# First attention layer: where GpSimd's low parts, the value load and the early expert parts stand

## The chip, the cores and the metric

The kernel runs on one core of a Trainium2 chip. The metric is the device time of one execution in microseconds (us). Five engines work side by side and wait for each other by semaphores: TensorE (PE), VectorE (DVE), ScalarE (ACT), GpSimd (POOL) and SyncE (SP, which here issues the DMA transfers).

## The reference

Two transformer layers over 2 sequences of 512 tokens, width 256. Each is attention, then a mixture of 16 experts. Only the first attention layer (16 heads of size 128) is touched by the change:

```python
x = x + _L0_attn_ref(_layernorm(x), ...)
# per head: q, k, v = x @ W + b; q, k = rotary(q), rotary(k)
scores = where(causal, q @ k.T / sqrt(128), 0)
max_v  = max(abs(scores), axis=-1)
attn_w = sign(scores) * exp(sign(scores) * scores - max_v)
attn   = attn_w / (sum(abs(attn_w)) + 1e-6)
out    = (attn @ v) @ W_O + b_O
x = x + _L0_ffn_ref(_layernorm(x), ...)      # experts, top 4 of 16, and a shared one
x = x + _L1_attn_ref(_layernorm(x), ...)
x = x + _L1_ffn_ref(_layernorm(x), ...)
```

## The kernel before

Matrix products are done in three passes over a high and a low part of each factor (`PARTS`): ScalarE rounds a float32 tile to its high part by a copy (`wqk_hi`, `wv_hi`, `wo_hi`, `ew_hi`), and GpSimd subtracts it from the raw tile to get the low part (`wqk_lo`, `wv_lo`, `wo_lo`, `ew_lo`).

The first layer is 32 heads (16 for each sequence), software-pipelined in steps i = -4 to 32. In step i TensorE projects q and k of head i+2 (L319), multiplies q by k for head i+1 (L330), applies the output weights for head i-1 (L343), transposes the weights `w` of head i (L357), projects v for two heads in halves (L370), and multiplies `w` by v for head i (L382). Steps 3 to 10 and 19 to 26 are run by a hardware loop with four steps in its body (`known(i)` is false there, since the step is a register); the others are written out one by one. After a written-out step, `a0_at_pe`, `a0_at_pool` and the like add work that belongs to that step alone.

Each engine runs its instructions strictly in program order; that order is written out by hand in `a0_pe`, `a0_act`, `a0_dve`, `a0_pool` and `a0_sp`. Around the change:

- GpSimd, `a0_pool`: L511 makes `wqk_lo` of head i+3, L518 the two products `q_sin` of the rotary step for head i+2 (from `q_sw`, q with neighbouring rows swapped by DMA), L525 masks `sabs` and `sgn` (absolute value and sign of the scores) for head i+1, L530 makes `wo_lo` of head i, L534 `wv_lo` of head i+4. In steps 28 to 30 `a0_at_pool` adds the low part `ew_lo` of an expert's weights, behind a wait for `rden`, and in step -3 the normalization's `rstd` of the second sequence (`ln_pool`, L265).
- VectorE, `a0_dve`: L468 and L474 finish the rotary step (`q_rot`), L479 takes the row maxima `nmax`, L486 multiplies `ex` by a mask and sums it into `den`, L458 adds the bias of v, L493 and L495 make `rden`, L499 the low part `z_lo`, L505 `w = ex * rden * sgn` in four pieces of 512, 384, 128 and 256 columns.
- SyncE, `a0_sp`: four swaps `q_sw`, then the loads of `wo_raw`, `wqk_raw` and `wv_raw`, each behind a wait for the low part that frees its one buffer.
- Before the steps, TensorE is kept warm with products of ones (L644), transposes `xn` (L277), the normalized input that VectorE writes at L242, and goes on to head 0.

## Time and profile before

| | us |
|---|---|
| median of 3 runs | 871.27 |
| lowest and highest | 868.90, 878.65 |
| the profiled execution, its own time | 869.21 |
| its span in the trace | 867.5 |

In the profiled execution TensorE is busy 95% of the span, VectorE 77%, ScalarE 60% and GpSimd 54%. A row of the time line is: start, length, engine, line, operation, output<-inputs, shapes, number of instructions merged, and in brackets how long the engine had been idle and what ended that. The granted clock is that of TensorE, where 1.00 is 2.4 GHz and 0.50 is 1.2 GHz.

### The profile page before, as it was taken

What the parts mean: (1) busy time and instruction counts of PE and PEld (TensorE: products, weight loads), DVE (VectorE), ACT (ScalarE), POOL (GpSimd) and SP (SyncE); (2) the same over time, 40 slices, a digit from 0 to 9 for tenths busy, and PEclk for the clock granted to TensorE, in tenths of its full rate; (3) what the DMA queues carried; (4) which work ended last, traced back from release to release, by engine and by line L of the source; (5) the groups of instructions that cost most, each with busy time, mean ns of one, the idle gap of its engine ahead of it and who ended that gap; (6) DMA issues with size and microseconds to landing.
All of it is one profiled execution on the core that took longest, in us unless ns stands there. A gap on an engine that the chain in (4) does not pass through costs nothing.

```text
span 867.5 us, 14790 instructions
## 1 busy us (share of the span) xinstructions
PE 826.4 (95%) x4549; PEld 626.9 (72%) x4549; DVE 670.3 (77%) x1350; ACT 522.9 (60%) x1106; POOL 469.1 (54%) x399
## 2 busy tenths in 40 slices
PE   8899999999989999889998999999999989999997
PEld 6678888777878888667787888664444447888886
DVE  5799999999999999998477865868788644675554
ACT  3778888786878888763644533336566665454442
POOL 3565555665666666532575766614210526656774
PEclk9999999999999999999999999999999999999999
DMA  4323332222432223211665457412441133334451
GB/s 148 101 97 99 98 97 97 96 83 73 148 97 99 97 97 98 68 48 49 201 226 166 140 164 271 155 57 63 142 136 53 56 99 92 122 122 141 152 161 65
DMA packets 57426, 99.20 MB, mean 114 GB/s; under 512 B 8272, under 2 KB 19024, under 8 KB 57360
## 3 DMA queue, kind: packets, MB, share of 16 engines
q1 hardware_dynamic: 57360, 98.39, 35.6%
q8 instruction: 33, 0.54, 0.3%
q14 instruction: 33, 0.27, 0.1%
HBM read 71.88 MB, written 9.57 MB: 94 GB/s over the span
## 4 chain that ended last, share of the span: by engine, by line
PE 63%; DVE 11%; issue 10%; POOL 9%; ACT 4%; DMA 2%; DVEq 0%; SPq 0%; ACTq 0%; POOLq 0%
PE ps L956 10%; PE ps L942 9%; PE ps L933 9%; PE ps L319 6%; PE ps L382 5%; PE ps L330 4%; POOL q_sin L518 3%; PE ps L343 3%; PE ps L370 3%; PE ps L1505 3%; PE ps L1624 3%; PE ps L357 2%; DVE w L505 2%; PE ps L1594 2%; DVE nm L1816 2%
## 5 line engine op out<-in xcount | busy, mean ns | idle before, releaser
L1080 POOL TENSOR_TENSOR ew_lo<-ew_raw,ew_hi 128x768 fp32r<-128x768 f32 x68 | 128.1, 1884 | 64.5 <-ACT ew_hi L1046 46.0
L1032 ACT ACTIVATE hid_hi<-guw 128x512 fp32r<-128x512 f32 x68 | 43.0, 632 | 156.6 <-POOL guw L1096 106.5
L1135 DVE TENSOR_TENSOR hid_lo<-guw,hid_hi 128x512 fp32r<-128x512 f32 x68 | 80.6, 1185 | 72.4 <-ACT hid_hi L1032 72.3
L1096 POOL TENSOR_TENSOR guw<-gu,cwb 128x512 f32<-128x512 f32 x61 | 80.4, 1319 | 91.5 <-issue 74.0
L505 DVE SCALAR_TENSOR_TENSOR w<-ex,rden,sgn 128x512 f32<-128x512 f32 (+3 forms) x128 | 103.2, 866 | 0.0
L1816 DVE TENSOR_REDUCE nm<-ps 128x1 f32<-128x512 f32 x128 | 81.3, 682 | 19.9 <-PE ps L1528 18.7
L1711 ACT ACTIVATE e<-ps 128x512 f32<-128x512 f32 x128 | 68.7, 602 | 36.8 <-PE ps L1624 36.6
L518 POOL TENSOR_TENSOR q_sin<-q_sw,sin 128x512 f32<-128x512 f32 x64 | 85.6, 1354 | 3.0 <-DMA q_sw<-q_in 2.7
L433 ACT ACTIVATE ex<-sabs,nmax 128x512 f32<-128x512 f32 (+3 forms) x128 | 61.5, 552 | 36.3 <-DVE nmax L479 36.3
L956 PE MATMUL ps<-ew_hi,hid_hi 128*128 128x256 f32 x272 | 78.4, 288 | 2.4 <-DVE hid_lo L1135 1.8
L956 PE MATMUL ps<-ew_hi,hid_lo 128*128 128x256 f32 x272 | 76.9, 283 | 0.0
L956 PE MATMUL ps<-ew_lo,hid_hi 128*128 128x256 f32 x272 | 76.9, 283 | 0.0
L382 PE MATMUL ps<-wT,v 128*128 128x512 f32 (+3 forms) x256 | 74.3, 433 | 1.0 <-ACT wT L418 1.0
L330 PE MATMUL ps<-q_rot 128*128 128x512 f32 (+3 forms) x256 | 74.2, 433 | 0.0
L511 POOL TENSOR_TENSOR wqk_lo<-wqk_raw,wqk_hi 128x512 fp32r<-128x512 f32 x32 | 43.9, 1371 | 55.8 <-ACT wqk_hi L398 55.8
L382 PEld LDWEIGHTS ps<-wT,v 128*128 128x128 f32 x256 | 46.3, 190 | 26.8 <-issue 16.6
L534 POOL TENSOR_TENSOR wv_lo<-wv_raw,wv_hi 128x256 fp32r<-128x256 f32 x32 | 23.8, 744 | 74.4 <-ACT wv_hi L448 74.4
L330 PEld LDWEIGHTS ps<-q_rot 128*128 128x128 f32 x256 | 43.3, 190 | 26.4 <-issue 15.4
L392 ACT ACTIVATE q_in<-ps,bqkv 128x512 f32<-128x512 f32 x64 | 43.7, 686 | 27.9 <-PE ps L319 27.4
L474 DVE TENSOR_TENSOR q_rot<-ps,q_sin 128x512 f32<-128x512 f32 x64 | 43.5, 686 | 22.1 <-POOL q_sin L518 19.9
L410 ACT ACTIVATE sgn<-ps 128x512 bf16<-128x512 f32 (+3 forms) x128 | 60.0, 469 | 0.0
L933 PE MATMUL ps<-xT_hi,ew_hi 128*128 128x512 f32 x136 | 55.8, 410 | 3.6 <-issue 3.6
(189 smaller groups left out, 2443.4 us busy)
## 6 DMA issues: line engine op xcount, KB each, us to landing
ew_raw<-in_ew SPq DMA_DIRECT2D x68, 384.0 KB, 3.4
q_sw<-q_in SPq DMA_DIRECT2D x128, 128.0 KB, 2.0
cwb<-cw_dram SPq DMA_DIRECT2D x61, 256.0 KB, 3.6
wqk_raw<-in_wqk SPq DMA_DIRECT2D x32, 256.0 KB, 2.9
wv_raw<-in_wv SPq DMA_DIRECT2D x32, 128.0 KB, 2.7
wo_raw<-in_wo SPq DMA_DIRECT2D x32, 128.0 KB, 2.2
qs<-stk_q SPq DMA_DIRECT2D x16, 256.0 KB, 3.7
ks<-stk_k SPq DMA_DIRECT2D x16, 256.0 KB, 4.3
```

What stands on the lines that cost most here:

```text
L330: pe.matmul(ps[:, bank, col:col + P * (qi + 1)], q_rot[:, par(1), 0, qi * P:(qi + 1) * P], q_rot[:, par(1), 1, 0:P * (qi + 1)], start=True ...
L382: last = pe.matmul(ps[:, 7, j * P:S], v0[:, slot_of(0), j, odd() * DH0:(odd() + 1) * DH0], wT[:, j, j * P:S], start=j == 0, stop=j == QT - ...
L505: dve.scalar_tensor_tensor(out=w[:, qi, ROW[qi]], in0=ex[:, qi, ROW[qi]], scalar=rden[:, qi:qi + 1], in1=sgn[:, par(1), qi, ROW[qi]], op0= ...
L518: pool.tensor_tensor(q_sin[:, t, :], q_sw[:, t, :], sin0[:, :], ALU.mult).then_inc(sem("q_sin"), 1)
L933: last = pe.matmul(ps[:, gu_pair(f, i)[0], :], ff[f].ew[pw][:, i % EW_SLOTS, c * P:(c + 1) * P], half_of((xT_hi, xT_lo)[px][:, c, :], h), ...
L942: last = pe.matmul(ps[:, gu_pair(f, i)[1], :], ff[f].ew[pw][:, i % EW_SLOTS, (DC + c) * P:(DC + c + 1) * P], half_of((xT_hi, xT_lo)[px][:, ...
L956: last = pe.matmul(ps[:, Y_BANK[f, h][t // 2], t % 2 * D:(t % 2 + 1) * D], ff[f].hid[px][:, i % 2, t * P:(t + 1) * P], ff[f].ew[pw][:, i % ...
L1080: pool.tensor_tensor(ff[f].ew[1][:, i % EW_SLOTS, :], ew_raw[:, i % RAW_SLOTS, :], fp(ff[f].ew[0][:, i % EW_SLOTS, :]), ALU.subtract).then ...
L1096: pool.tensor_tensor(ff[f].guw[:, i % 2, :], ff[f].gu[:, i % 2, :], ff[f].cwb[:, r % CWB_SLOTS, :], ALU.mult).then_inc(sem("guw"), 1)
L1135: dve.tensor_tensor(ff[f].hid[1][:, i % 2, :], ff[f].guw[:, i % 2, :], fp(ff[f].hid[0][:, i % 2, :]), ALU.subtract).then_inc(sem("hid_lo"), 1)
L1711: act.activation(e1[:, s % 2 * HEADS + j, :], ps[:, S_BANK[n % S_BANKS], :], ACT.Exp, scale=SCALE1).then_inc(sem("e1"), 1)
L1816: dve.tensor_reduce(nm1[:, quad % 2, col:col + 1], ps[:, BANK_OF["max", n], :], AX.X, ALU.max, negate=True).then_inc(sem("max"), 1)
```

## The change

Five moves, no arithmetic is added or removed. (1) In the two hardware loops `wqk_lo` goes from first place in GpSimd's step to behind the two masks. (2) There, `wo_lo` gets a further wait, for the four sums `den` of head i+1. (3) In the loops, SyncE issues the load of `wv_raw` before those of `wo_raw` and `wqk_raw`. (4) At the start, `wv_lo` and `wqk_lo` of head 0 wait until the four `xn` tiles of the first sequence are written, and `rstd` of the second sequence goes ahead of `wv_lo` of head 1. (5) In steps 28 to 30 an expert's `ew_lo` goes from the end of the step, behind a wait for `rden`, to right behind the masks, without that wait, and ahead of `wo_lo` (in step 28 also ahead of `rstd`, `gw_lo` and a memset).

```diff
--- before.py
+++ after.py
@@ -504,12 +504,20 @@
                 for qi in QORDER:
                     dve.scalar_tensor_tensor(out=w[:, qi, ROW[qi]], in0=ex[:, qi, ROW[qi]], scalar=rden[:, qi:qi + 1],
                                              in1=sgn[:, par(1), qi, ROW[qi]], op0=ALU.mult, op1=ALU.mult).then_inc(sem("w"), 1)
-        def a0_pool(pool, i):
+        def wqk_low(pool, i):
             if valid(i + 3, N0):
                 n = i + 3
+                if known(i) and i == -3:
+                    pool.wait_ge(sem("xn"), QT)
                 wait(pool, "wqk_hi", n + 1)
                 pool.tensor_tensor(wqk[1][:, :, :, :], wqk_raw[:, :, :, :], fp(wqk[0][:, :, :, :]),
                                    ALU.subtract).then_inc(sem("wqk_lo"), 1)
+
+        def a0_pool(pool, i):
+            if known(i):
+                wqk_low(pool, i)
+            if known(i) and i == -3:
+                ln_pool(pool, 0, (1,))
             if valid(i + 2, N0):
                 n = i + 2
                 for t in range(2):
@@ -524,19 +532,32 @@
                     diag = t[:, :, S - P:S]
                     pool.affine_select(out=diag, in_=diag, compare_op=ALU.is_ge, fill=0.0, base=0,
                                        pattern=[[0, QT], [-1, P]], channel_multiplier=1).then_inc(sem("causal"), 1)
+            if not known(i):
+                wqk_low(pool, i)
+            if known(i) and N0 - 4 <= i <= N0 - 2:
+                ew_low(pool, 0, i - (N0 - 4))
             if valid(i, N0):
                 n = i
                 wait(pool, "wo_hi", n + 1)
+                if not known(i):
+                    wait(pool, "den", QT * (n + 2))
                 pool.tensor_tensor(wo[1][:, :], wo_raw[:, :], fp(wo[0][:, :]), ALU.subtract).then_inc(sem("wo_lo"), 1)
             if valid(i + 4, N0):
                 n = i + 4
                 wait(pool, "wv_hi", n + 1)
+                if known(i) and i == -4:
+                    pool.wait_ge(sem("xn"), QT)
                 pool.tensor_tensor(wv[1][:, slot_of(4), :, odd(), :], wv_raw[:, :, :], fp(wv[0][:, slot_of(4), :, odd(), :]),
                                    ALU.subtract).then_inc(sem("wv_lo"), 1)
 
         def a0_sp(sp, i):
             def head(n):
                 return n % H0 if known(n) else n - batch[0] * H0
+
+            def load_wv(sp, n):
+                src = a["wv0"][head(n)]
+                wait(sp, "wv_lo", n)
+                sp.dma_start(wv_raw[:, :, :], src).then_inc(sem("wv_ld"), 16)
 
             if valid(i + 2, N0):
                 n = i + 2
@@ -544,6 +565,8 @@
                     wait(sp, "q_ev", of_pair(n + 1, t))
                     for o in range(2):
                         sp.dma_start(q_sw[o:P:2, t, :], q_in[1 - o:P:2, t, :]).then_inc(sem(f"swap{t}"), 16)
+            if not known(i):
+                load_wv(sp, i + 4)
             if valid(i, N0):
                 n = i
                 src = a["wo0"][head(n)]
@@ -554,9 +577,8 @@
                 src = a["wqk0"][head(n)]
                 wait(sp, "wqk_lo", n)
                 sp.dma_start(wqk_raw[:, :, :, :], src).then_inc(sem("wqk_ld"), 16)
-                src = a["wv0"][head(n)]
-                wait(sp, "wv_lo", n)
-                sp.dma_start(wv_raw[:, :, :], src).then_inc(sem("wv_ld"), 16)
+                if known(i):
+                    load_wv(sp, n)
 
         batch = [0]
         quarter = [0]
@@ -610,7 +632,6 @@
 
         def a0_at_pool(pool, i):
             if i == -3:
-                ln_pool(pool, 0, (1,))
                 pool.wait_ge(sem("tab0"), 80)
             if H0 - 5 <= i < H0 - 1:
                 t = 2 * (i - (H0 - 5))
@@ -627,9 +648,6 @@
             if i == N0 - 4:
                 ln_pool(pool, 1, (0,))
                 gw_low(pool, 0)
-            if N0 - 4 <= i <= N0 - 2:
-                pool.wait_ge(sem("rden"), i + 2)
-                ew_low(pool, 0, i - (N0 - 4))
             if i == N0 - 2:
                 ew_low(pool, 0, 3)
             if i == N0:
```

GpSimd in the hardware loop, first of its four steps, before (L511 is `wqk_lo` of head i+3; rows of L217 set registers for the waits):

```order
L511 TENSOR_TENSOR wqk_lo<-wqk_raw,wqk_hi 128x512 [waits wqk_hi]
L217 ISA
L217 ISA [waits swap0]
L518 TENSOR_TENSOR q_sin<-q_sw,sin_66 128x512 [waits q_rot]
L217 REGISTER_ALU [waits swap1]
L518 TENSOR_TENSOR q_sin<-q_sw,sin_66 128x512 [waits q_rot]
L217 ISA
L525 AFFINE_SELECT sabs<-sabs 128x4x128 [waits sgn]
L525 AFFINE_SELECT sgn<-sgn 128x4x128
L530 TENSOR_TENSOR wo_lo<-wo_raw,wo_hi 128x256 [waits wo_hi]
L217 REGISTER_ALU
L534 TENSOR_TENSOR wv_lo<-wv_raw,wv_hi 128x2x128 [waits wv_hi]
```

and now:

```order
L526 TENSOR_TENSOR q_sin<-q_sw,sin_66 128x512 [waits q_rot]
L217 REGISTER_ALU [waits swap1]
L526 TENSOR_TENSOR q_sin<-q_sw,sin_66 128x512 [waits q_rot]
L217 ISA
L533 AFFINE_SELECT sabs<-sabs 128x4x128 [waits sgn]
L533 AFFINE_SELECT sgn<-sgn 128x4x128
L217 REGISTER_ALU
L513 TENSOR_TENSOR wqk_lo<-wqk_raw,wqk_hi 128x512 [waits wqk_hi]
L217 ISA [waits wo_hi]
L544 TENSOR_TENSOR wo_lo<-wo_raw,wo_hi 128x256 [waits den]
L217 REGISTER_ALU
L550 TENSOR_TENSOR wv_lo<-wv_raw,wv_hi 128x2x128 [waits wv_hi]
```

`wqk_lo` moved from ahead of the swaps' products to behind the masks, and `wo_lo` waits for `den` too. SyncE in the same step, before:

```order
L546 DMA q_sw<-q_in 64x512 [waits q_ev]
L546 DMA q_sw<-q_in 64x512
L217 REGISTER_ALU
L551 ISA [waits wo_lo]
L551 DMA wo_raw<-in_wo 128x256
L217 REGISTER_ALU
L556 ISA [waits wqk_lo]
L556 DMA wqk_raw<-in_wqk 128x512
L559 ISA [waits wv_lo]
L559 DMA wv_raw<-in_wv 128x256
```

and now:

```order
L567 DMA q_sw<-q_in 64x512 [waits q_ev]
L567 DMA q_sw<-q_in 64x512
L217 REGISTER_ALU
L560 ISA [waits wv_lo]
L560 DMA wv_raw<-in_wv 128x256
L217 REGISTER_ALU
L574 ISA [waits wo_lo]
L574 DMA wo_raw<-in_wo 128x256
L579 ISA [waits wqk_lo]
L579 DMA wqk_raw<-in_wqk 128x512
```

The value load moved ahead of the two others; the load of `wqk_raw` is last and waits for the `wqk_lo` that now comes later. GpSimd in steps 28 and 29, written out, before (L1080 is `ew_lo` of experts 0 and 1):

```order
L525 AFFINE_SELECT sgn<-sgn 128x4x128
L530 TENSOR_TENSOR wo_lo<-wo_raw,wo_hi 128x256 [waits wo_hi]
L265 TENSOR_TENSOR rstd<-vareps,minus_half 128x4 [waits ln_var]
L1085 TENSOR_TENSOR gw_lo<-gw_raw,gw_hi 128x32 [waits gw_hi]
L1087 MEMSET runs 128x640
L1080 TENSOR_TENSOR ew_lo<-ew_raw,ew_hi 128x768 [waits ew_hi_act,rden]
L518 TENSOR_TENSOR q_sin<-q_sw,sin_66 128x512 [waits q_rot,swap0]
L518 TENSOR_TENSOR q_sin<-q_sw,sin_66 128x512 [waits q_rot,swap1]
L525 AFFINE_SELECT sabs<-sabs 128x4x128 [waits sgn]
L525 AFFINE_SELECT sgn<-sgn 128x4x128
L530 TENSOR_TENSOR wo_lo<-wo_raw,wo_hi 128x256 [waits wo_hi]
L1080 TENSOR_TENSOR ew_lo<-ew_raw,ew_hi 128x768 [waits ew_hi_act,rden]
```

and now:

```order
L533 AFFINE_SELECT sgn<-sgn 128x4x128
L1098 TENSOR_TENSOR ew_lo<-ew_raw,ew_hi 128x768 [waits ew_hi_act]
L544 TENSOR_TENSOR wo_lo<-wo_raw,wo_hi 128x256 [waits wo_hi]
L265 TENSOR_TENSOR rstd<-vareps,minus_half 128x4 [waits ln_var]
L1103 TENSOR_TENSOR gw_lo<-gw_raw,gw_hi 128x32 [waits gw_hi]
L1105 MEMSET runs 128x640
L526 TENSOR_TENSOR q_sin<-q_sw,sin_66 128x512 [waits q_rot,swap0]
L526 TENSOR_TENSOR q_sin<-q_sw,sin_66 128x512 [waits q_rot,swap1]
L533 AFFINE_SELECT sabs<-sabs 128x4x128 [waits sgn]
L533 AFFINE_SELECT sgn<-sgn 128x4x128
L1098 TENSOR_TENSOR ew_lo<-ew_raw,ew_hi 128x768 [waits ew_hi_act]
L544 TENSOR_TENSOR wo_lo<-wo_raw,wo_hi 128x256 [waits wo_hi]
```

In each step `ew_lo` moved up to the masks and lost its wait for `rden`; in step 28 it is also ahead of L265, L1103 and L1105 (`rstd`, `gw_lo`, memset).

## Rows read from the trace of the kernel before

**Rows 1.** Windows: length, busy us of PE, PEld, DVE, ACT, POOL; clock, DMA, GB/s.

```profile
260.00:310.00 50.00, 50.00 (x279) 40.27 (x278) 47.65 (x111) 40.82 (x101) 29.48 (x31) 1.00 0.29 95
369.30:372.80 3.50, 3.50 (x18) 3.50 (x19) 3.50 (x7) 1.83 (x5) 1.40 (x3) 0.52 0.02 9
```

**Rows 2.** TensorE's waits, 40 to 400 us: total, how many, longest.

```profile
PE ps L357 <- DVE w L505: 11.0, 6, 3.5
```

**Rows 3.** Time line of TensorE, steps 5 and 6.

```profile
96.65 0.59 PE L382 MATMUL ps<-wT,v 128*128 128x512 f32 x1
98.73 0.49 PE L319 MATMUL ps<-xT_hi,wqk_hi 128*128 128x512 f32 x1
107.70 0.59 PE L382 MATMUL ps<-wT,v 128*128 128x512 f32 x1
```

**Rows 4.** Time line of VectorE, the same step.

```profile
96.27 0.69 DVE L474 TENSOR_TENSOR q_rot<-ps,q_sin 128x512 f32<-128x512 f32 x1 [0.56 <-POOL q_sin L518]
96.88 1.65 DVE L479 TENSOR_REDUCE nmax<-sabs 128x1 f32<-128x512 f32 x4
101.85 2.96 DVE L505 SCALAR_TENSOR_TENSOR w<-ex,rden,sgn 128x512 f32<-128x512 f32 x4
```

**Rows 5.** Time line of GpSimd, the same step.

```profile
93.46 2.72 POOL L518 TENSOR_TENSOR q_sin<-q_sw,sin 128x512 f32<-128x512 f32 x2
96.13 0.64 POOL L525 TENSOR_SCALAR_AFFINE_SELECT sabs<-sabs 128x512 f32<-128x512 f32 x1
97.32 0.73 POOL L530 TENSOR_TENSOR wo_lo<-wo_raw,wo_hi 128x256 fp32r<-128x256 f32 x1
...
103.18 1.34 POOL L511 TENSOR_TENSOR wqk_lo<-wqk_raw,wqk_hi 128x512 fp32r<-128x512 f32 x1 [2.07 <-ACT wqk_hi L398]
```

**Rows 6.** One line: ns min/median/max, starts; the last piece of w at two places.

```profile
L505 DVE SCALAR_TENSOR_TENSOR w<-ex,rden,sgn x1: 1506/1506/1506, 103.3 to 103.3; 128x256 f32<-128x256 f32 x1
...
L505 DVE SCALAR_TENSOR_TENSOR w<-ex,rden,sgn x1: 471/471/471, 380.9 to 380.9; 128x256 f32<-128x256 f32 x1
```

**Rows 7.** One line or tile: a step's second swap, and GpSimd's lengths, 40 to 352.

```profile
L546 SPq DMA_DIRECT2D q_sw<-q_in x2: 465/530/596, 102.6 to 103.1; - x2
DMA to landing us min/median/max: 1.9/2.0/2.1
...
L511 POOL TENSOR_TENSOR wqk_lo<-wqk_raw,wqk_hi x27: 1281/1357/1652, 46.8 to 341.1; 128x512 fp32r<-128x512 f32 x27
```

**Rows 8.** Time line of the start, TensorE and VectorE.

```profile
9.86 0.61 PE L644 MATMUL ps<-ones_r 128*128 128x512 f32 x2
10.79 1.07 PE L277 MATMUL ps<-ident,xn 128*128 128x128 f32 x8 [0.32 <-DVE xn L242]
...
7.88 2.76 DVE L242 TENSOR_SCALAR xn<-x,meanvar,rstd 128x256 f32<-128x256 f32 x4 [1.20 <-POOL rstd L265]
16.30 1.38 DVE L242 TENSOR_SCALAR xn<-x,meanvar,rstd 128x256 f32<-128x256 f32 x4 [1.13 <-POOL rstd L265]
```

**Rows 9.** Time line of steps 28 to 30: VectorE, GpSimd, TensorE.

```profile
363.93 5.23 DVE L505 SCALAR_TENSOR_TENSOR w<-ex,rden,sgn 128x512 f32<-128x512 f32 x4
369.09 2.00 DVE L242 TENSOR_SCALAR xn<-x,meanvar,rstd 128x256 f32<-128x256 f32 x4
378.20 3.16 DVE L505 SCALAR_TENSOR_TENSOR w<-ex,rden,sgn 128x512 f32<-128x512 f32 x4
...
363.52 1.83 POOL L1080 TENSOR_TENSOR ew_lo<-ew_raw,ew_hi 128x768 fp32r<-128x768 f32 x1 [3.66 <-DVE rden L495]
366.35 2.53 POOL L518 TENSOR_TENSOR q_sin<-q_sw,sin 128x512 f32<-128x512 f32 x2 [1.00 <-DMA q_sw<-q_in]
...
377.79 1.84 POOL L1080 TENSOR_TENSOR ew_lo<-ew_raw,ew_hi 128x768 fp32r<-128x768 f32 x1 [4.65 <-DVE rden L495]
...
369.22 1.19 PE L357 MATMUL ps<-ident,w 128*128 128x128 f32 x5 [3.46 <-DVE w L505]
...
381.42 1.31 PE L357 MATMUL ps<-ident,w 128*128 128x128 f32 x10 [1.25 <-DVE w L505]
```

## The prediction

> **What bounds the kernel now.** The whole change lies in the first layer, so I read that stage. The busy windows come first: over 50 us inside the second hardware loop TensorE is busy for all 50 us at clock 1.00, while VectorE has 47.65 and GpSimd 29.48 [rows 1]. The time line of TensorE gives the step: from the product with v of one head to that of the next it is 107.70 - 96.65 = 11.05 us [rows 3]. So in the loops (16 of 32 heads) TensorE has no hole that a faster partner could close. Its waits from 40 to 400 us come next: 11.0 us in six waits for `w`, the longest 3.5 us [rows 2]. Since the loops have no idle time, these lie in the steps that are written out. The reader is to see that VectorE is nearly full too, and that it is slowed by GpSimd at two kinds of place. In the loop the last piece of `w` takes 1506 ns, against 471 ns for the same piece in step 30 [rows 6]; it starts at 103.3, just behind the start of `wqk_lo` at 103.18, and ends 0.3 us after it [rows 5, 6]. In step 28 the four pieces of `w` take 5.23 us beside `ew_lo` and the two `q_sin`, and TensorE then waits 3.46 us for them; in step 30 they take 3.16 us beside an `ew_lo`, and the wait is 1.25 us [rows 9]. Where GpSimd is already in a subtraction or product, such a piece of VectorE's simply stands until that has ended.
>
> **The terms.** *Loops, moves 1 to 3.* Moving `wqk_lo` away from `w` saves VectorE 1.51 - 0.47 = 1.04 us a step [rows 6], and `q_sin` no longer stands behind it, so most of the 0.56 us wait of `q_rot` goes too [rows 4]. But TensorE is full [rows 1], so I cost this gain at nothing: VectorE is only earlier by 1 to 1.6 us at a point where TensorE is not waiting. Nor is the lead carried out of the loop, since the first written-out step starts again with `wqk_lo` in its old place and `q_rot` waits there for the swap. The price to look for is the new deadline. The first product of the next step needs this step's `wqk_lo`, which used to end at 103.18 + 1.34 = 104.5, some 5 us early [rows 5]. Now the chain is: the second pair of swaps is issued at 103.1 at the latest and lands 2.1 us on, at 105.2 [rows 7]; `q_sin` 2.72 / 2 = 1.36 us; two masks of 0.64 us; `wqk_lo` 1.36 us [rows 5, 7]. That is 105.2 + 1.36 + 1.28 + 1.36 = 109.2, and TensorE's next first product is due at 98.73 + 11.05 = 109.8 [rows 3]. Slack 0.6 us: tight, and enough. It costs nothing unless the chain is longer; if `wqk_lo` takes its longest, 1.65 us [rows 7], 0.3 us is still left. Queued behind `wqk_lo` are only `wo_lo` and `wv_lo`; on SyncE the load of `wqk_raw` waits for it with the next step's swaps behind, but these are due two us later. The value load ahead of that of `wo_raw` delays `wo_hi` by one issue, some 0.5 us [rows 7], in a gap that ScalarE has before the exponentials. So the loops give 0; bounds 0 and, if the chain is 0.5 us late in every step, 16 x 0.5 = +8 us.
>
> The row maxima show no slowing beside GpSimd: 1.65 us for the four with `wo_lo` at 97.32 inside them [rows 4, 5]. The Trainium skill (SBUF — State Buffer, "Who interferes with whom") says the same of `tensor_reduce`, and says against the change that a VectorE operation with two SBUF inputs, which the sums of `den` are, contends with GpSimd; no row here has one beside a GpSimd read. By it the first `den` sum would stand for the last 0.3 to 0.4 us of `wqk_lo`, each step, inside VectorE's new lead, and the sum would stay as it is.
>
> *Start, move 4.* `xn` takes 2.76 us beside the two low parts and 1.38 us alone [rows 8], so VectorE gains 1.38 us. TensorE does not: it runs its warming products until 9.86 + 0.61 = 10.47 and has waited only 0.32 us when the transposes start at 10.79 [rows 8]. The gain is capped there: 0.32 us, and I take 0.35 us, with the semaphore's own delay. `wqk_lo` of head 0 then ends some 2 us after `xn`, before head 0's first product. Behind it the loads for head 1 leave 1.5 us later, and `wv_lo` of head 1 now runs beside the second `xn`, which can eat the gain: bounds 0 and -0.6 us.
>
> *Steps 28 to 30, move 5.* `ew_lo` of expert 0 now stands beside `q_rot` and the row maxima, which cost nothing above, and `w` of head 29 loses it. A clean `w` is 2.96 - 1.51 for the first three pieces and 0.47 for the last, 1.9 us, and 2.05 with the overlaps of neighbours counted out [rows 4, 6]. Starting at 363.93 it ends at 366.0, just before the first `q_sin` at 366.35 [rows 9]: 5.23 - 2.05 = 3.2 us earlier. Not all is kept. What is late next is `xn` of the next normalization, four pieces that took 2.00 us [rows 9] and now fall beside the two `q_sin` (2.53 us from 366.35): I let two pieces pass before them and two stand behind one product each, so that `xn` ends near 369.8 in place of 371.1, and 1.3 us is kept. Then `w` of head 30 loses its `ew_lo`: 3.16 - 2.05 = 1.1 us. Together 2.4 us at the transposes that now start at 381.42 [rows 9], with TensorE's 1.25 us wait gone and the rest from its earlier inputs. Behind that point TensorE is hardly idle, so the shift stays to the end. `rstd`, `gw_lo` and the memset, now behind `ew_lo`, fall beside the `den` sums and may hold them 0.4 us; then the last piece of `w` meets `q_sin` and the 1.3 us go. Bounds: -1.1 us (only head 30's piece) and -3.5 us. The upper one adds the clock: behind the 3.46 us hole the granted clock is 0.52 over 3.5 us [rows 1], where TensorE was at 1.2 GHz; without the hole that work takes some 1.6 us less, of which VectorE's chain lets only a part through.
>
> **Sum.** 0 - 0.35 - 2.4 = -2.75 us on the profiled execution's own 869.2: 866.5. That execution is 2.1 us below the median of 871.27; the runs before spread from 868.9 to 878.65. With 868.5 from the median and 866.5 from the profile I forecast 867.6 us, 0.4% below the median.
>
> **The rivals.**
> - *The loop's new deadline is missed (slower).* For it: the chain above is a ring (first product, `q_in`, swap, `q_sin`, masks, `wqk_lo`, next first product), so any time over the 0.6 us slack is paid in all 16 steps. Swaps that land 3 us after their issue, now that another load goes out right behind them, or products slowed beside VectorE, would do it. Against it: swaps landed within 1.9 to 2.1 us with a load behind them too, and the lengths of masks and products are from rows in which VectorE was busy [rows 5, 7]. It decides from 0.6 us; 0.3 us more gives 16 x 0.3 = +4.8, or 866.5 + 4.8 = 871.3 us; at 1.2 us late in all it gives 876.
> - *The end's gain goes again.* `w` of head 29 still meets `q_sin`, `xn` stands behind it, and only the 1.1 us of head 30 or less is left: 868.5 us. For it: a margin of only 366.35 - 366.0 = 0.35 us. Against it: the wait for `rden` held `ew_lo` until 363.52, exactly ahead of `w`, and that is surely gone.
> - *The loops do follow VectorE.* If the 11.05 us were set by VectorE's ring (47.65 of 50 us busy) and TensorE's fullness only modelled, 0.56 us or more a step would come off: 16 x 0.56 = 9 us, 858 us. Against it: TensorE shows no wait in the loops, where the other steps do show theirs [rows 1, 2], and VectorE has idle time that it could have used [rows 4].
>
> **How the numbers follow.** Forecast 0.66; missed deadline 0.14 (of it 0.05 by enough for over 1%); end's gain gone 0.16; loops follow VectorE 0.04. The range goes down to 863.5 (profile's level with the end at -3.5 and 2 us of run noise) and up to 873 (median's level with +4.8). Over 1%, 8.7 us, is about what a measurement here can tell from no change: faster 0.05, same 0.89, slower 0.06.
>
> **What would show it.** TensorE's step in the loops at 11.05 us with no wait for `wqk_lo`; the last piece of `w` in the loops near 0.47 us and no 0.56 us wait of `q_rot`; the first `xn` at 1.4 us and the transposes at about 10.5; `w` of head 29 near 2.05 us, the 3.46 us hole and the 0.5 clock behind it gone, the transposes of head 30 near 379. A TensorE wait for `wqk_lo` in the loop would prove the first rival; a `w` of over 3 us in step 28 the second; a step under 11.0 us the third.

## The result, and the profile after

| | us |
|---|---|
| kernel before, median of 14 runs beside it | 872.04 (868.72 to 878.79) |
| changed kernel, median of 14 runs | 868.65 (863.83 to 874.63) |
| ratio changed / before | 0.9939, 95% interval 0.9911 to 0.9967 |
| the changed kernel's profiled execution, its own time | 865.04 (before: 869.21) |
| its span in the trace | 863.3 (before: 867.5) |

A second set of runs of the changed kernel gave a ratio of 0.9927 (0.9886 to 0.9968). (Below, "the rounds" are such repeated timed runs of a kernel beside the kernel before.) It is 0.6% faster, within 1%, as forecast (867.6 us, 863.5 to 873.0).

The page of the changed kernel, its busy times, and two of its costliest groups (busy us, mean ns of one, idle time before and its releaser):

```profile
PE 828.1 (96%) x4549; PEld 627.4 (73%) x4549; DVE 646.3 (75%) x1350; ACT 525.3 (61%) x1106; POOL 465.8 (54%) x399
...
L526 POOL TENSOR_TENSOR q_sin<-q_sw,sin 128x512 f32<-128x512 f32 x64 | 83.5, 1312 | 51.7 <-DMA q_sw<-q_in 50.4
...
L505 DVE SCALAR_TENSOR_TENSOR w<-ex,rden,sgn 128x512 f32<-128x512 f32 (+3 forms) x128 | 79.0, 680 | 0.0
```

VectorE does the same 1350 instructions in 646.3 us, where it took 670.3 us, and all of that is `w`, which took 103.2 us. GpSimd waits 50.4 us for the swaps, where it waited 2.7 us. So 24 us came off one engine, and 4 us off the kernel.

The same views as ahead of the prediction. Windows (length, busy us of PE, PEld, DVE, ACT, POOL; clock, DMA, GB/s) of the loop and of the place behind `w` of head 29, which answer to [rows 1], and one more at 242.6 us; then TensorE's waits from 40 to 400 us, which answer to [rows 2]:

```profile
260.00:310.00 50.00, 50.00 (x280) 40.22 (x279) 42.28 (x107) 40.66 (x100) 28.49 (x32) 1.00 0.29 98
365.80:369.30 3.50, 3.50 (x23) 2.75 (x21) 3.50 (x4) 1.84 (x6) 3.50 (x5) 1.00 0.56 183
242.60:245.90 3.30, 3.30 (x17) 3.30 (x16) 3.30 (x8) 2.69 (x8) 0.80 (x2) 0.50 0.00 0
```

```profile
PE ps L357 <- DVE w L505: 4.6, 5, 2.2
...
PE ps L319 <- POOL wqk_lo L513: 0.5, 1, 0.5
```

In the loop VectorE is busy 42.28 of 50 us and not 47.65, and TensorE still 50.00. The waits for `w` fell from 11.0 to 4.6 us; 4.6 us of that are the two of heads 29 and 30. Another 1.4 us, at head 14 (2.18 to 0.76), does not repeat: the second trace of the changed kernel waits 2.18 us there. One wait is new in kind: 0.5 us for `wqk_lo`, the deadline that the change made.

The loop in the time line (start, length, engine, line, operation, tiles, shapes, count, idle before and releaser), TensorE, then GpSimd, then VectorE, which answer to [rows 3 to 5]:

```profile
98.52 0.49 PE L319 MATMUL ps<-xT_hi,wqk_hi 128*128 128x512 f32 x1 [0.48 <-POOL wqk_lo L513]
107.46 2.32 PE L382 MATMUL ps<-wT,v 128*128 128x512 f32 x8
109.54 0.49 PE L319 MATMUL ps<-xT_hi,wqk_hi 128*128 128x512 f32 x1
118.50 2.32 PE L382 MATMUL ps<-wT,v 128*128 128x512 f32 x8
```

```profile
107.62 1.27 POOL L513 TENSOR_TENSOR wqk_lo<-wqk_raw,wqk_hi 128x512 fp32r<-128x512 f32 x1
```

```profile
101.53 1.93 DVE L505 SCALAR_TENSOR_TENSOR w<-ex,rden,sgn 128x512 f32<-128x512 f32 x4
...
106.56 0.69 DVE L474 TENSOR_TENSOR q_rot<-ps,q_sin 128x512 f32<-128x512 f32 x1 [0.78 <-POOL q_sin L526]
```

The four pieces of `w` take 1.93 us, not 2.96, and `q_rot` waits for `q_sin` as before: VectorE's gain has become a wait for the swaps. From 107.46 to 118.50 the step is 11.04 us. `wqk_lo` ends at 107.62 + 1.27 = 108.89, and the first product that needs it starts at 109.54: slack 0.65 us. One step earlier a swap was late, and TensorE waited 0.48 us.

The end, steps 28 to 30, VectorE, GpSimd and TensorE, which answer to [rows 9]:

```profile
363.05 1.94 DVE L505 SCALAR_TENSOR_TENSOR w<-ex,rden,sgn 128x512 f32<-128x512 f32 x4
364.90 3.33 DVE L242 TENSOR_SCALAR xn<-x,meanvar,rstd 128x256 f32<-128x256 f32 x4
...
375.34 1.93 DVE L505 SCALAR_TENSOR_TENSOR w<-ex,rden,sgn 128x512 f32<-128x512 f32 x4
```

```profile
365.38 2.69 POOL L526 TENSOR_TENSOR q_sin<-q_sw,sin 128x512 f32<-128x512 f32 x2 [4.13 <-DMA q_sw<-q_in]
```

```profile
370.80 1.09 PE L277 MATMUL ps<-ident,xn 128*128 128x128 f32 x8 [0.85 <-DVE q_rot L474]
374.71 0.67 PE L330 MATMUL ps<-q_rot 128*128 128x256 f32 x2 [1.09 <-DVE v L458]
377.33 1.31 PE L357 MATMUL ps<-ident,w 128*128 128x128 f32 x10 [0.16 <-DVE w L505]
```

`w` of head 29 takes 1.94 us in place of 5.23, and behind it the granted clock stays at 1.00 where it was 0.52. The 3.46 us hole is gone; smaller waits of 0.85, 1.09 and 0.16 us stand where it was. The transposes of head 30 start at 377.33, not 381.42.

### Where the time went, trace by trace

Single traces differ by more than the change is worth, so I cut each at the same places. The table gives, for every kernel of this study, how much later (+) or earlier (-) than in the trace of before each stretch made the product with v (L382). "Start" is that of head 0; "loop 1" is what the products of heads 4 to 11 add (there a late `wqk_lo` of steps 3 to 10 is felt), "11 to 19" the eight heads behind it, "loop 2" heads 20 to 27, "end" heads 29 to 31, and "rest" is the span less all of these, the 470 us behind (from the rounded span, so good to 0.1 us).

| kernel | start | loop 1 | 11 to 19 | loop 2 | end | rest | span |
|---|---|---|---|---|---|---|---|
| changed kernel | -0.93 | +0.69 | -0.31 | +0.23 | -3.76 | -0.11 | -4.2 |
| changed kernel, second trace | -0.65 | +0.25 | +2.96 | +0.20 | -3.74 | +7.25 | +6.3 |
| loops_only | +0.66 | +1.47 | +0.10 | +0.15 | +0.91 | +1.98 | +4.2 |
| start_only | -0.60 | +1.12 | +3.29 | +0.87 | -0.67 | +6.88 | +10.9 |
| end_only | +0.84 | +1.16 | +0.29 | 0.00 | -2.95 | -1.46 | -2.3 |
| end_no_wait | -0.18 | +2.91 | -2.15 | 0.00 | -2.43 | +1.64 | -0.2 |
| no_den_wait | -0.74 | +0.49 | +3.63 | +0.27 | -3.17 | +2.11 | +2.6 |
| no_load_first | -0.70 | +7.71 | +1.29 | +7.63 | -1.78 | +1.79 | +17.1 |
| late_full | -0.51 | +11.57 | -0.98 | +8.54 | -2.64 | +0.04 | +16.2 |
| late_half | -0.43 | +9.38 | +0.17 | +8.97 | -3.67 | +4.54 | +18.9 |
| all_steps | -0.90 | +0.35 | +2.53 | +0.90 | -3.78 | +3.29 | +2.4 |
| all_steps0 | -0.73 | +0.88 | +4.27 | 0.00 | -3.76 | +0.28 | +1.9 |
| carried_on | -0.63 | +0.03 | +0.38 | +0.54 | -3.76 | +3.41 | 0.0 |

(What is missing to the span lies in heads 1 to 3 and 28: -1.07 us in loops_only and +0.95 in all_steps0 in the first, +1.15 in no_load_first in the second, under 0.2 elsewhere.) The columns "11 to 19" and "rest" vary by 6 and 9 us among kernels that are alike there: these are chance, of two kinds shown further down. "Start" has chance in it too: `rstd` starts anywhere from 6.39 to 6.86 us. The loops of before happen to be the best of all: the three other traces with the old order in them are 1.2 to 2.9 us behind it (both loops together), the seven with the new order and no delay 0.45 to 1.6 us. So the new order has no loss there that shows. The second trace of the changed kernel is of its longest execution in that set, 875.50 us beside a median of 869.20. The column "end" is -3.74 to -3.78 in the five traces of kernels that have all five moves and loops without delay. The verdicts on small effects below are read from this table and the rounds together.

### The profile page after: what moved, and what is told of

It reads as the page before. It is cut to its first block, busy times and chain, and to the rows that moved or that the text cites. A ratio compares the mean times of both kernels' runs of the same rounds, so it can differ in the third digit from the quotient of the medians.

```text
span 863.3 us, 14805 instructions
## 1 busy us (share of the span) xinstructions
PE 828.1 (96%) x4549; PEld 627.4 (73%) x4549; DVE 646.3 (75%) x1350; ACT 525.3 (61%) x1106; POOL 465.8 (54%) x399
## 4 chain that ended last, share of the span: by engine, by line
PE 64%; issue 10%; POOL 10%; DVE 10%; ACT 4%; DMA 2%; SPq 0%; DVEq 0%; POOLq 0%; ACTq 0%
PE ps L974 10%; PE ps L951 10%; PE ps L960 9%; PE ps L319 6%; PE ps L382 5%; PE ps L330 4%; POOL q_sin L526 3%; PE ps L343 3%; PE ps L370 3%; PE ps L1642 2%; PE ps L1523 2%; PE ps L357 2%; PE ps L1612 2%; POOL wqk_lo L513 2%; DVE nm L1834 2%
## 5 line engine op out<-in xcount | busy, mean ns | idle before, releaser
L526 POOL TENSOR_TENSOR q_sin<-q_sw,sin 128x512 f32<-128x512 f32 x64 | 83.5, 1312 | 51.7 <-DMA q_sw<-q_in 50.4
L505 DVE SCALAR_TENSOR_TENSOR w<-ex,rden,sgn 128x512 f32<-128x512 f32 (+3 forms) x128 | 79.0, 680 | 0.0
L382 PE MATMUL ps<-wT,v 128*128 128x512 f32 (+3 forms) x256 | 74.5, 433 | 1.0 <-ACT wT L418 1.0
L382 PEld LDWEIGHTS ps<-wT,v 128*128 128x128 f32 x256 | 46.5, 191 | 26.9 <-issue 16.7
L408 ACT ACTIVATE sabs<-ps 128x512 f32<-128x512 f32 (+3 forms) x128 | 58.7, 459 | 0.0
L1642 PE MATMUL ps<-qs,ks 50*128 50x512 f32 x128 | 51.5, 466 | 6.3 <-ACT e L1729 6.3
```

The costliest lines, as they stand in the source:

```text
L382: last = pe.matmul(ps[:, 7, j * P:S], v0[:, slot_of(0), j, odd() * DH0:(odd() + 1) * DH0], wT[:, j, j * P:S], start=j == 0, stop=j == QT - ...
L505: dve.scalar_tensor_tensor(out=w[:, qi, ROW[qi]], in0=ex[:, qi, ROW[qi]], scalar=rden[:, qi:qi + 1], in1=sgn[:, par(1), qi, ROW[qi]], op0= ...
L526: pool.tensor_tensor(q_sin[:, t, :], q_sw[:, t, :], sin0[:, :], ALU.mult).then_inc(sem("q_sin"), 1)
L1642: pe.matmul(ps[:, S_BANK[n % S_BANKS], :], ks[rows, slot_at, kt * P:(kt + 1) * P], qs[rows, slot_at, :], start=True, stop=True).then_inc(s ...
```

## The experiments

### The parts alone: loops_only, start_only, end_only

The edits are the moves of the change, each put alone into the kernel before: moves 1 to 3; move 4; move 5. In short, for GpSimd:

```diff
 loops_only:  +            if not known(i):
              +                wqk_low(pool, i)          # and wo_lo's wait for den, load_wv first on SyncE
 start_only:  +                if known(i) and i == -3:
              +                    pool.wait_ge(sem("xn"), QT)
 end_only:    +            if known(i) and N0 - 4 <= i <= N0 - 2:
              +                ew_low(pool, 0, i - (N0 - 4))
```

> Moves 1 to 3 alone: in the loops the masks come before wqk_lo, wo_lo waits for den, and the value load goes first. Start and end as in the kernel before. Theory E (the gain is made at the end and the start, the loops give nothing): step of the loops 11.04 us as before, the last piece of w near 0.48 us, and a time of 0 to +1.5 us against the kernel before (ratio 1.000 to 1.002), where the plus is a late swap that now shows as a wait of TensorE for wqk_lo, 0.3 to 1.3 us a time. Theory L (the whole change gains in the loops and in the steps behind them, since VectorE and GpSimd are relieved; in the trace of after step 14 alone is 1.4 us shorter): -1.5 to -3 us (ratio 0.9965 to 0.998).

> Move 4 alone: the first normalization stands ahead of wqk_lo and wv_lo of head 0. Theory E: xn 1.38 us in place of 2.76, the first transposes up to 0.5 us earlier, so -0.3 to -0.6 us in all (ratio 0.9993 to 0.9997), under what the rounds can tell from nothing. If the 0.93 us by which the trace of after leads at step 0 were all of this move and kept: -0.9 us (ratio 0.999).

> Move 5 alone: ew_lo of the second layer's experts right behind the masks in steps 28 to 30, without its wait for rden. Theory E: w of head 29 about 2 us in place of 5.2, no hole of TensorE of over 2 us there and no granted clock near 0.5 behind it; the shift made between steps 28 and 31 is -3 to -4 us and stays to the end (ratio 0.9955 to 0.9965). Theory L: at most -1.1 us, the piece of head 30 alone (ratio 0.9987).

Measured against the kernel before: loops_only 0.9987 (0.9959 to 1.0014), start_only 1.0028 (0.9995 to 1.0060), end_only 0.9952 (0.9925 to 0.9980). Only the end is told from nothing, and it carries nearly the whole ratio of 0.9939. The product of the three is 0.9967, which the intervals allow.

loops_only, TensorE in the loop: the step is 11.04 us but for one late swap, which costs 0.95 us.

```profile
99.51 0.49 PE L319 MATMUL ps<-xT_hi,wqk_hi 128*128 128x512 f32 x1 [0.95 <-POOL wqk_lo L511]
```

That is not a net price, for the old order pays for a late swap too. In end_no_wait, whose loops are those of before, three swaps of step 5 landed up to 3.9 us after their issue; `q_sin` was late and `w` stood beside it, and TensorE waited 2.69 us for `w`. Landing times of that step's swaps, then TensorE's wait:

```profile
L546 SPq DMA_DIRECT2D q_sw<-q_in x4: 464/548/1567, 90.0 to 91.9; - x4
...
DMA to landing us min/median/max: 2.0/3.3/3.9
...
107.84 1.31 PE L357 MATMUL ps<-ident,w 128*128 128x128 f32 x10 [2.69 <-DVE w L505]
```

start_only, `xn` and the transposes behind it: 1.38 us, and no wait of TensorE for `xn`.

```profile
6.71 1.01 POOL L265 TENSOR_TENSOR rstd<-vareps,minus_half 128x4 f32<-128x4 f32 x1 [5.81 <-DVE vareps L236]
...
7.76 1.38 DVE L242 TENSOR_SCALAR xn<-x,meanvar,rstd 128x256 f32<-128x256 f32 x4 [1.20 <-POOL rstd L265]
...
10.18 1.03 PE L277 MATMUL ps<-ident,xn 128*128 128x128 f32 x8
```

From `rstd` to the transposes it is 10.18 - 6.71 = 3.47 us here and 9.87 - 6.39 = 3.48 us in the changed kernel, against 3.96, 3.95 and 3.97 us in before, end_only and end_no_wait. So move 4 is worth 0.48 us. That the rounds of start_only lean the other way (1.0028) I can't explain from its trace, where the losses lie in "11 to 19" and "rest", far behind the edit (and that trace is of an execution of 880.14 us, near its longest, with a median of 873.89); the interval just includes 1.

end_only, VectorE and TensorE at the end:

```profile
352.99 2.96 DVE L505 SCALAR_TENSOR_TENSOR w<-ex,rden,sgn 128x512 f32<-128x512 f32 x4
366.11 1.94 DVE L505 SCALAR_TENSOR_TENSOR w<-ex,rden,sgn 128x512 f32<-128x512 f32 x4
...
377.95 0.67 PE L330 MATMUL ps<-q_rot 128*128 128x256 f32 x2 [2.18 <-DVE v L458]
```

Theory E holds: `w` of head 29 takes 1.94 us and the stretch gains 2.95 us. The rest up to 3.76 us comes with the loops' moves: `w` of head 28, made in step 27, the first behind the loop, takes 2.96 us here and 1.93 us in the changed kernel, and TensorE's wait for `v` is 2.18 us here and 1.09 us there. What a short `w` of head 28 is worth shows with and without move 5, in the time from the product with v of head 28 to that of head 29. With move 5 it is 11.81 us here and 11.19 us in the changed kernel. Without it, it is 16.63 us in before and 15.94 us in loops_only, whose `w` of head 28 takes 1.93 us. So 0.6 to 0.7 us each time. (start_only has the short `w` too, by chance, behind a `w` of head 27 that took 4.01 us: 15.88 us, hence its -0.67. loops_only gains the 0.69 us and loses more to a second fall of the clock at 384.1 us, hence its +0.91.)

### Is it the wait or the place? end_no_wait

```diff
             if N0 - 4 <= i <= N0 - 2:
-                pool.wait_ge(sem("rden"), i + 2)
                 ew_low(pool, 0, i - (N0 - 4))
```

> The kernel before, and only the wait of ew_lo for rden in steps 28 to 30 taken out; ew_lo keeps its place at the end of GpSimd's step. In the trace of before GpSimd is idle from 359.86 to 363.52 us in step 28, until rden. Without the wait ew_lo takes 1.83 us from 359.9, beside the den sums, and is gone by 361.7, before w at 363.93. If the loss sat in the wait: w of head 29 is about 2 us in place of 5.2, less what the den sums lose (up to 1.3 us), and the gain between the products with v of steps 28 and 31 is 2 to 4 us, as with move 5 whole (2.96 us in its own trace). If the place behind the masks is what counts: under 1.5 us.

Measured: ratio 0.9991 (0.9956 to 1.0026); in its trace the end gains 2.43 us. GpSimd and VectorE there:

```profile
360.43 1.85 POOL L1079 TENSOR_TENSOR ew_lo<-ew_raw,ew_hi 128x768 fp32r<-128x768 f32 x1
...
361.42 1.41 DVE L486 SCALAR_TENSOR_TENSOR ex<-sgn,ex 128x512 f32<-128x512 bf16 x1
...
365.26 1.93 DVE L505 SCALAR_TENSOR_TENSOR w<-ex,rden,sgn 128x512 f32<-128x512 f32 x4
...
373.22 1.94 DVE L486 SCALAR_TENSOR_TENSOR ex<-sgn,ex 128x512 f32<-128x512 bf16 x1
```

By the trace, 2.43 of end_only's 2.95 us sit in the wait for `rden` alone: taking it out makes `w` 1.93 us. The place behind the masks adds the rest, since in the old place `ew_lo` meets the first `den` sum, which then takes 1.41 and 1.94 us in place of 0.68. (No run moved `ew_lo` and kept its wait.) The rounds do not show the gain, though they leave room for it (-3.8 to +2.3 us); the evidence for this split is the trace.

### The new deadline made later: late_full and late_half

```diff
+                if known(i):
+                    pool.sem_inc(sem("extra"), 1)
+                else:
+                    pool.tensor_tensor(wqk[1][:, :, :, :], wqk_raw[:, :, :, :], fp(wqk[0][:, :, :, :]),
+                                       ALU.subtract).then_inc(sem("extra"), 1)
+                wait(pool, "extra", n + 1)
                 pool.tensor_tensor(wqk[1][:, :, :, :], wqk_raw[:, :, :, :], fp(wqk[0][:, :, :, :]),
                                    ALU.subtract).then_inc(sem("wqk_lo"), 1)
```

late_half has `[:, :, 0:2, :]` in the added subtraction. That slice was meant as half, but this dimension has only two entries (256 columns in chunks of 128), so it is the whole tile. The two kernels do the same, and what was expected of the second was not put to the test; it is a repetition.

> The changed kernel with its new deadline made late on purpose: in each of the 16 loop steps the subtraction of wqk_lo is made twice, one behind the other, so it ends 1.36 us and a semaphore's delay of about 0.1 us later. The slack read from the trace of after is 109.54 - 108.89 = 0.65 us. If the chain swap, q_sin, masks, wqk_lo is a ring with that slack, every step is 1.45 - 0.65 = 0.8 us longer, 11.85 in place of 11.04, with a wait of TensorE for wqk_lo in each: 16 x 0.8 = +13 us against the changed kernel, some +8 against the one before (ratio to before 1.009). If the time hangs on TensorE's own fullness and the wait is absorbed (products run closer behind it): less than +4 us against the changed kernel.

> The same delay as in the run with the doubled subtraction, in half the size: in the 16 loop steps half of wqk_lo (128x256) is made first and then all of it, so it ends some 0.64 + 0.08 = 0.72 us later. With the whole one doubled wqk_lo ended 1.28 + 0.08 + 0.31 (its second pass met a den sum) = 1.67 us later and the steps grew by 1.07 us: slack 0.60 us. If the slack is a threshold: 0.72 - 0.60 = 0.1 us a step, 11.1 to 11.2 in place of 11.04, +1.5 to +3 us against the changed kernel (ratio to the kernel before 0.996 to 0.998). If there is no slack and the time follows the delay in proportion: 0.72 / 1.67 x 1.07 = 0.46 us a step, +7 us (ratio 1.002).

Measured: 888.31 us, ratio 1.0195 (1.0156 to 1.0235), and 886.01 us, 1.0152 (1.0117 to 1.0186): 17 to 20 us over the changed kernel. late_full, waits of TensorE from 40 to 400 us, then GpSimd, TensorE and a `den` sum of one step:

```profile
PE ps L319 <- POOL wqk_lo L519: 16.4, 16, 2.9
...
137.98 1.28 POOL L516 TENSOR_TENSOR wqk_lo<-wqk_raw,wqk_hi 128x512 fp32r<-128x512 f32 x1
139.34 1.59 POOL L519 TENSOR_TENSOR wqk_lo<-wqk_raw,wqk_hi 128x512 fp32r<-128x512 f32 x1
...
141.06 0.49 PE L319 MATMUL ps<-xT_hi,wqk_hi 128*128 128x512 f32 x1 [0.83 <-POOL wqk_lo L519]
153.15 0.49 PE L319 MATMUL ps<-xT_hi,wqk_hi 128*128 128x512 f32 x1 [0.81 <-POOL wqk_lo L519]
...
139.74 1.61 DVE L486 SCALAR_TENSOR_TENSOR ex<-sgn,ex 128x384 f32<-128x384 bf16 x1
```

The ring is real: 16 waits, one in each loop step, and a step of 153.15 - 141.06 = 12.09 us. The delay was 0.2 us more than I had reckoned, as the second subtraction met a `den` sum and took 1.59 us: 140.93 - 139.26 = 1.67 us later than one alone. 1.67 less the 12.09 - 11.04 = 1.05 us that the step grew leaves a slack of 0.62 us, beside the 0.6 of the prediction and the 0.65 read from the trace. That the cost starts at that point, with nothing below it, has only the unhindered steps of the changed kernel behind it.

### Moves 2 and 3 taken back: no_den_wait and no_load_first

```diff
 no_den_wait:
-                if not known(i):
-                    wait(pool, "den", QT * (n + 2))
 no_load_first:
-            if not known(i):
-                load_wv(sp, i + 4)
...
-                if known(i):
-                    load_wv(sp, n)
+                load_wv(sp, n)
```

> The changed kernel without move 2's wait of wo_lo for den in the loops: wo_lo then follows wqk_lo at once, and stands beside the den sums, which have two SBUF inputs. A den piece that meets the 0.73 us of wo_lo stands up to that long, in VectorE's lead of over 1 us, so w starts at most 0.7 us later and TensorE sees nothing: 0, -0.5 to +1 us against the changed kernel. If VectorE's lead were not there: +0.5 us x 16 = +8 us.

> The changed kernel without move 3: in the loops the value load is issued last again, behind the load of wqk_raw, which waits for the wqk_lo that move 1 made late. In the run with wqk_lo behind the masks in the written-out steps too, where move 3 was not made, the load of wv_raw was issued at 212.10 us right behind a wqk_lo that ended at 211.70, landed at 214.76, and wv_lo ran at 215.28 to 216.55 beside w; TensorE's product with v fell back by 0.56 to 0.79 us in steps 13, 15, 16 and 19. If that is what a missing move 3 costs: +0.5 to +0.8 us in each of the 16 loop steps, +8 to +13 us against the changed kernel, ratio to the kernel before 1.003 to 1.009, with waits of TensorE for w or wqk_lo in every step. If those losses came from the additions to x that share these steps: no change against the changed kernel (ratio 0.994 to 0.995), the step of the loops 11.04 us.

(In this expectation and the next two a step is counted by the product in which its `wqk_lo` is felt, one more than its i.) Measured: no_den_wait 0.9947 (0.9917 to 0.9977), not told from the kernel with the wait (0.9939, 0.9927). In the loops `wo_lo` follows `wqk_lo` at once and holds a `den` sum for 0.5 us (1.08 us for 384 columns in place of 0.55), inside VectorE's lead, and TensorE sees nothing of it. But the lead is then shorter at the loop's end, and `w` of head 28 meets `wqk_lo` again:

```profile
354.43 2.96 DVE L505 SCALAR_TENSOR_TENSOR w<-ex,rden,sgn 128x512 f32<-128x512 f32 x4
```

Its end gains 3.17 us and not 3.74 to 3.78, and the time from head 28 to head 29 is 11.79 us, as in end_only. By this one trace move 2 is worth some 0.6 us, at the end and not in the loops; the rounds are too coarse to tell.

no_load_first: 887.63 us, ratio 1.0182 (1.0119 to 1.0245), more than the upper end expected. Move 3 is what makes move 1 free. Its SyncE, ScalarE and GpSimd in one loop step:

```profile
136.71 0.34 SPq L577 DMA_DIRECT2D wqk_raw<-in_wqk  x1
137.26 0.33 SPq L560 DMA_DIRECT2D wv_raw<-in_wv  x1
140.79 2.41 SPq L567 DMA_DIRECT2D q_sw<-q_in  x4
...
139.77 0.42 ACT L448 ACTIVATE wv_hi<-wv_raw 128x256 fp32r<-128x256 f32 x1 [1.95 <-DMA wv_raw<-in_wv]
140.09 1.25 ACT L392 ACTIVATE q_in<-ps,bqkv 128x512 f32<-128x512 f32 x2
...
135.15 1.27 POOL L513 TENSOR_TENSOR wqk_lo<-wqk_raw,wqk_hi 128x512 fp32r<-128x512 f32 x1
```

The load of `wqk_raw` waits for `wqk_lo`, the load of `wv_raw` stands behind it on SyncE, and ScalarE waits 1.95 us for it at `wv_hi` with `q_in` queued behind. So a ring of its own closes: `wqk_lo`, the two loads, `wv_hi`, `q_in`, swap, `q_sin`, masks, `wqk_lo`. It takes 12.1 us a step, 1.05 us over TensorE's 11.04 (the next `wqk_lo` starts at 147.24).

### More of the same, to find a faster kernel: after_again, all_steps, all_steps0, carried_on

after_again is the changed kernel unedited. all_steps makes move 1 alone in the written-out steps i = 11 to 18 too, all_steps0 from step 0 on. carried_on makes moves 1 to 3 in steps 11 to 15 and shifts the additions to x away from `w`:

```diff
 all_steps:
-            if known(i):
+            if known(i) and not 3 <= i <= N0 - 6:
                 wqk_low(pool, i)
...
-            if not known(i):
+            if not known(i) or 3 <= i <= N0 - 6:
                 wqk_low(pool, i)
 carried_on:
+        def late(i):
+            return not known(i) or 11 <= i <= 15
...
+            if late(i):
+                wqk_low(pool, i)
+            if known(i) and H0 - 5 <= i < H0 - 1:
+                x_bo(pool, i)                        # was at the end of the step, L636
```

> The changed kernel as it is, beside the variants of this call. From the trace of after: 3 to 5 us under the kernel before (ratio 0.994 to 0.9965). Its profile shows which of the small shifts repeat. Theory E: -3 to -5 us between the products with v of steps 28 and 31, in this trace too. The 1.4 us that step 14 gave in the trace of after is a matter of phase and the 3.4 us of slow clock at 242 us a matter of chance; both may be absent.

> The changed kernel, and wqk_lo behind the masks in the written-out steps 3 and 12 to 19 too. In the trace of after TensorE waits there for w 0.66 us in step 12, 0.76 in step 14 and 2.19 in step 18, where w stands beside wqk_lo and the two q_sin. Theory E (where TensorE does wait for w, a faster w comes through): these waits go but for what the additions to x cost in step 18, so -2 to -3 us against the changed kernel, ratio to the kernel before 0.991 to 0.993. Theory L (only the sum of GpSimd's work counts there): no change against it. If the new deadline is missed in those steps, whose GpSimd work is 1.3 us longer in steps 11 to 14, 17 and 18: up to +1 us.

> The same, from step 0 on. In the trace of after TensorE waits 1.55 us for w at 36.85 and 0.86 us at 48.97, and the last pieces of w there take 1.49 us beside wqk_lo against 0.48 alone. Theory E: another 1 + 0.86 = 1.9 us off where these waits go, -4 to -5 us against the changed kernel in all, ratio to the kernel before 0.989 to 0.991. The risk is the deadline of the first steps, where the loads are late: a wait of TensorE for wqk_lo of up to 1 us in each of steps 0 to 2 would eat it.

> An attempt at a faster kernel: the changed kernel with moves 1, 2 and 3 together also in the written-out steps 11 to 15 (step 16 and later keep the old order, since SyncE's long row of expert loads stands in step 16), the additions of the output bias to x in steps 11 to 14 put between wqk_lo and wo_lo, and those of steps 17 and 18 between wo_lo and wv_lo, where GpSimd is idle (232.47 to 234.79 us in the trace of after), in place of behind wv_lo, where they meet w. Theory E: the waits for w of steps 12 and 14 (1.4 to 3.0 us in the three traces of the changed kernel and its near copy) go, that of step 18 falls from 2.2 to under 1 us, and no step falls back by 0.5 us or more: -2.5 to -4 us against the changed kernel, ratio to the kernel before 0.989 to 0.992. If the written-out steps have no slack for the new deadline even with the value load first: waits for wqk_lo of 0.3 to 0.6 us in steps 12 to 16, no gain against the changed kernel.

Measured: 0.9927 (0.9886 to 0.9968), 0.9997 (0.9963 to 1.0031), 1.0016 (0.9979 to 1.0053), 0.9971 (0.9930 to 1.0012). All three attempts fell short of the changed kernel, all_steps and all_steps0 by 3.3 and 5.4 us (872.48 and 874.63 beside 869.20 us), carried_on by less than its interval can tell. all_steps, TensorE's waits one by one in these steps:

```profile
188.15 0.50 PE L319 MATMUL ps<-xT_hi,wqk_hi 128*128 128x512 f32 x1 [0.39 <-POOL wqk_lo L513]
195.12 1.31 PE L357 MATMUL ps<-ident,w 128*128 128x128 f32 x10 [0.37 <-DVE w L505]
...
232.93 0.87 PE L357 MATMUL ps<-ident,w 128*128 128x128 f32 x6 [2.37 <-ACT sgn L410]
237.97 0.50 PE L319 MATMUL ps<-xT_hi,wqk_hi 128*128 128x512 f32 x1 [0.58 <-POOL wqk_lo L513]
```

The waits for `w` did shrink, as theory E said, but the new ring, here without move 3, puts waits for `wqk_lo` and `sgn` in their place. The 2.37 us stand behind step 16, in which SyncE also issues the expert weights' loads: the loads of `wqk_raw` and `wv_raw`, now later, are issued right ahead of them and land 4.8 us after their issue, and ScalarE waits 3.82 us for `wv_raw` with `q_in` behind. all_steps0 has a wait of 4.26 us for `wqk_lo` at one product, and that is another thing: the four swaps of that step landed 3.9 to 6.4 us after their issue and GpSimd sat idle for 6.83 us. (Such swaps are looked at in the last section.) carried_on has no wait for `wqk_lo` in steps 12 to 16 beyond 0.54 us. Of the waits for `w` that it was to remove, that of step 12 is gone, but 1.66 us are left in step 14, 0.66 us in step 16, and the wait of step 18 stayed at 2.33 us: its addition to x held the `den` sum instead (1.39 us). Its "11 to 19" is +0.38 us, within the scatter; its rounds show no gain over the changed kernel. No kernel that was run is told to be faster than the changed one; end_only, no_den_wait and carried_on are not told from it either.

## Why the prediction was right

- *Loops at 0: right.* The step is 11.04 us with VectorE at 42.28 of 50 us. TensorE's fullness is the bound there; the rival in which the loops follow VectorE would have made it under 11.0, and loops_only 9 us faster; it is 0.9987.
- *The last piece of `w`, 1.04 us a step: right* (1.93 in place of 2.96 us for the four). Where I was wrong is "most of the 0.56 us wait of `q_rot` goes": it waits 0.78 us in the row above and 25.0 us over the whole, where it waited 19.9 us, since `q_sin` follows the swaps and the swaps follow TensorE.
- *The new deadline, slack 0.6 us: right* in size (0.65 in the trace, 0.62 by late_full) and in kind, a ring. The rival in which it is missed is a real mechanism with the price that I gave it, and it did not happen but where a swap was late (0.48 us once in the first trace).
- *Move 3 as a small cost on `wo_hi`: the wrong side of it.* I priced what the value load delays and not what it would delay if left where it was. no_load_first lies 19 us (887.63 - 868.65) over the changed kernel. The number was right only because the change had the move.
- *Move 2:* nothing in the loops, as counted; some 0.6 us at the end by one trace, which the prediction did not have.
- *Start, -0.35 us: measured -0.48.* The cap that I read was 0.16 us too low. The ten last warming products start at `rstd` in both kernels; what differs is what follows them. In the changed kernel the row of the last three ends at 9.18 + 0.84 = 10.02, and yet the transposes start at 9.87:

```profile
9.18 0.84 PE L662 MATMUL ps<-ones_r 128*128 128x512 f32 x3
9.87 0.27 PE L277 MATMUL ps<-ident,xn 128*128 128x128 f32 x1
```

So the end in such a row lies some 0.16 us behind the point at which the next product can start, and the 0.32 us wait, counted from that end, left this out: 0.32 + 0.16 = 0.48. The rest of the -0.93 us in the table is `rstd` itself, which started 0.44 us earlier in that trace, and no row shows why: it starts at 6.39 to 6.74 us in the ten traces with move 4 and at 6.68 to 6.86 in the four without.
- *End, -2.4 us: measured -3.76* in the trace, -2.95 for move 5 alone. `w` of head 29 was right (3.2 us forecast, 5.23 - 1.94 = 3.29), and so was head 30 (1.1 us forecast, 3.16 - 1.93 = 1.23). The term that was mis-sized is what is kept of the first: 1.3 us by the prediction, 2.5 by the trace, where `xn` ended at 368.23, or 368.56 on the clock of before (the general shift is 0.33 us), and not at 369.8. That has two parts. VectorE started that `w` another 0.55 us earlier (363.05 + 0.33 = 363.38, not 363.93), since the loop's lead was carried out of it: "Nor is the lead carried out of the loop" is the sentence that failed. And `xn` beside `q_sin` took 3.33 us behind the `w`, where the prediction gave it 369.8 - 366.0 = 3.8. The sum, 2.5 + 1.2 = 3.7 us, is what the trace shows.
- *The clock behind the hole: right in direction.* Behind the 3.46 us hole of before it was 0.52 [rows 1]; there is no hole and no fall at that place in the changed kernel. What the clock's share of the 3.76 us is, no run separates; a fall at another place of the end cost 1.0 to 1.6 us (last section).
- *The `den` sums beside GpSimd.* By the Trainium skill (SBUF — State Buffer, "Who interferes with whom") an operation of VectorE with two SBUF inputs contends with a GpSimd instruction that reads SBUF. The traces agree: a `den` sum took 1.41 and 1.94 us beside `ew_lo`, and 1.61 us for 384 columns beside `wqk_lo`, against 0.68 and 0.55 us alone. As counted, it cost nothing in the changed kernel, where the first sum starts only 0.15 us before `wqk_lo` ends.

The sum was -2.75 us; the terms measured one by one are 0, -0.5 and -3.8, together -4.3 us, and the profiled execution moved by 4.17 us. The medians of the rounds moved by 3.4 us. That agreement is partly luck. The profiled execution has 0.44 us of an early `rstd` and +0.92 us from the loops in it, which no term had; with the -0.31 us of "11 to 19" they nearly cancel. And the forecast of 867.6 us lay between the 868.5 that the sum gives from the median and the 866.5 that it gives from the profile: the end came out 1.4 us better than forecast, and the measured 868.65 us is still on the higher side.

## What to carry to other kernels

Freeing a full partner engine moves the end only where the bounding engine waits for it: here 24 us less on VectorE gave 4 us, nearly all at one hole of 3.46 us, and by the traces some 2.4 us of that by dropping one semaphore wait. When work is moved late, follow its buffer: the load that waits for it, the loads queued behind that one, and who waits for those; moving `wqk_lo` without moving the value load would have cost 2%. And a slack of 0.6 us that holds in a loop is none in the straight-line code around it: there the same order came out 3 to 5 us slower without the load moved, late swaps included, and with no gain that shows when it was moved.
